# Scores in two passes: the keys as whole-number rows, their scale in the exponential, the maximum's shift brought in by two queues

## The chip, the cores and the metric

One core of one Trainium2 chip. The number is the device time of one execution in microseconds (us), the median over several runs. The engines are TensorE (PE, with its weight load PEld), VectorE (DVE), ScalarE (ACT), GpSimd (POOL) and SyncE (SP), each working through its own instructions in order; SP and ACT can also issue DMAs.

## The reference

32 sequences of 128 tokens out of an alphabet of 28 go through three layers. Only the attention matters here:

```python
h = tok_ref(ids, mask, ...)               # embedding, window feature over 3 tokens, linear map, layernorm
x = _layernorm(h)                         # [B=32, S=128, D=256]
q, k, v = x @ Wq + bq, x @ Wk + bk, x @ Wv + bv        # 16 heads of 64
attn = softmax(q @ k.T / sqrt(64))
y = x + (attn @ v) @ Wo + bo
h = h + layernorm(y, eps=1e-3) * gamma + beta
h = h + ffn_ref(_layernorm(h), ...)       # router over 16 experts, top 2, gelu experts
```

## The kernel before

A token's layernormed row depends only on which token it is and on what stands beside it. So each token is a short row u of 64 numbers: 28 one-hot entries and 28 window shares (together `nb`), both scaled by `r12`, the token's own inverse root, and a few constant columns. `ub` holds these rows transposed for all 32 sequences, as a f16 value and its f16 rest (`ub[:, b, 0]`, `ub[:, b, 1]`), twice over, on partitions 0 to 63 and 64 to 127 (halves `ab` = 0, 1). Queries are `gp` times `ub`, again as value and rest, `qh` and `ql`. Row `SHIFT` of `qh` holds minus the maximum of the query's scores, and row `SHIFT` of the keys' `ub` holds ones, so the shift comes with the product.

The kernel has three stages. Stage 1 builds tables, roots and `ub`. Stage 2 is the attention: one turn `i` of its loop works on several sequences at once. Stage 3 is the feed-forward part. The order on each engine is written out by hand and kept by semaphores. In a turn of stage 2:

- PE: `residual(i)` (L1278), `turn(i+1, 0)`, `values(i+1, 1)`, logits, `q_rows`, `score_cols(i+2, 1)` (L1238), `maxima_cols(i+3)` (L1309), `turn(i+1, 1)`, `q_rows`, `output(i+1, 0)`, `values(i+2, 0)`, `score_rows(i+4, 0)`, `score_cols(i+3, 0)`, `x_cols(i)` (L1287), `output(i+1, 1)`, `score_rows(i+4, 1)`.
- ACT: `max_row(i+3)` (L972: the negated maxima of 16 heads into `mrow`), `exps(i+2, 3)` (L953), `q_hi(i+4, 1)` (L944), `context_hi`, `exps(i+2, 2)`, `probs_hi` twice (L959), `exps(i+3, 1)`, `x_hi(i)` (L976), `exps(i+3, 0)`, `probs_hi` twice, `y_squares(i+1)` (L992).
- POOL: `var_y(i)` (L851, after `y_squares`), `root_y`, `probs_lo`, `h2`, `probs_lo`, `var_x`, `x_rows` (the last is L882, writing `xc`), then `probs_lo` twice.
- SP: waits for `mrow`, then two DMAs (L836), one for each half `ab`, bring 8 heads' maxima each into row `SHIFT` of `qh`.

`score_cols` makes the scores of 4 heads for each half, in three passes: `ub[.., 0]` by `qh`, `ub[.., 0]` by `ql`, `ub[.., 1]` by `qh`. A pass is two matmuls of 512 columns, one on each half of the rows. For `hf` = 0 it waits for the shift's DMAs and for `exps(b-1, 2)` and `exps(b-1, 3)`; `x_cols(b)` waits for `xc`. `exps` gives its bias `ln_r[:, b]` from SBUF and its scale as a constant.

Of the kernel before, what the change touches and what calls it, by code (L numbers as in the profile page):

```python
# [34 lines left out]
V = 28  # L35
# [6 lines left out]
R2, ONE, SHIFT = 2 * V, 2 * V + 1, 2 * V + 2  # L42
ONE_HI, UV = R2 + 2, R2 + 4
# [48 lines left out]
def build(nc, d, out):  # L92
    with ExitStack() as ctx:
# [28 lines left out]
        u_top, u_rest, nk = uh[:, 0], ul[:, 0], uh[:, 1]  # L122
# [45 lines left out]
        uf = sb1("uf", [P, B, UD])  # L168
# [18 lines left out]
        nk_step = sem("nk_step")  # L187
# [12 lines left out]
        UT_BANKS = [psum[n] for n in (2, 3, 6, 7)]  # L200
        TABLE_BANKS = [psum[4], psum[5], psum[4]]
# [16 lines left out]
        with nc.Block() as block:  # L218
# [30 lines left out]
            @block.gpsimd  # L249
            def _(pool):  # L250
                nc.gpsimd.memset(lhs_t[:], 0.0).then_inc(cleared, 1)
                nc.gpsimd.memset(row1[:], 0.0).then_inc(cleared, 1)
                nc.gpsimd.memset(tg[:], 0.0).then_inc(cleared, 1)
                nc.gpsimd.memset(ex[:], 0.0).then_inc(cleared, 1)
                pool.wait_ge(cleared, CLEARED["row_0"])
                nc.gpsimd.memset(row1[:, 0:V], 1.0).then_inc(cleared, 1)
                nc.gpsimd.memset(nb[:, :, 2 * V:UD], 0.0).then_inc(cleared, 1)
                nc.gpsimd.memset(tt[:], 0.0).then_inc(cleared, 1)
                nc.gpsimd.memset(uf[:, :, R2:UD], 0.0).then_inc(cleared, 1)
                nc.gpsimd.memset(mhalf[:], -0.5)  # L260
# [4 lines left out]
                nc.gpsimd.memset(uf[:, :, ONE:SHIFT + 1], 1.0).then_inc(cleared, 1)  # L265
                pool.wait_ge(nt_ready, 4)
# [12 lines left out]
                pool.wait_ge(nk_step, 3)  # L279
                for n, src in ((R2, s1), (ONE_HI, s12)):  # L280
                    nc.gpsimd.tensor_scalar(column(n), src[:], 1.0, 0.0, ALU.mult, ALU.add).then_inc(nk_step, 1)
                pool.wait_ge(nk_step, 5)
                for n, src in ((R2, s1), (ONE_HI, s12)):
                    nc.gpsimd.tensor_tensor(column(n + 1), src[:], column(n), ALU.subtract)

            @block.scalar
            def _(act):
# [15 lines left out]
                act.wait_ge(n_ok, 2)  # L303
                nc.scalar.activation(nk[:, :, 0:2 * V], nb[:, :, 0:2 * V], ACT.Copy)
# [82 lines left out]
            def _(dve):  # L387
# [29 lines left out]
                for n in range(2):  # L417
# [26 lines left out]
                                      twice(psum[7][:, 0:2 * KC * UD].rearrange("p (x u) -> p x u", u=UD))).then_inc(mt_ok, 1)  # L444
                dve.wait_ge(cs_ok, 1)
# [9 lines left out]
                                               op0=ALU.mult, op1=ALU.subtract).then_inc(mr_ok, 1)  # L455

# [91 lines left out]
            def _(pe):  # L548
# [34 lines left out]
                keep_going(15, psum[0][:, 0:FREE])  # L583
# [8 lines left out]
                keep_going(6, psum[0][:, 0:FREE])  # L592
# [57 lines left out]
                def gram():  # L650
                    pe.wait_ge(qkv_ok, 4)
                    for h in range(H):
                        k0 = K * (h % 2)
                        c = (h // 8 * 4 + h // 2 % 2 * 2 + h // 4 % 2) * UD
                        mm = nc.tensor.matmul(psum[h % 2][0:UD, c:c + UD], qkv_t[k0:k0 + K, 0, h // 2, :],
                                              qkv_t[k0:k0 + K, 1, h // 2, :], start=True, stop=True)
                        if h >= H - 2:
                            mm.then_inc(g_ready, 1)

                def z_part(n):  # L660
                    if n == 0:
# [18 lines left out]
                quads(3)  # L680
                table(1)
# [26 lines left out]
        in_cd, gate, g_exp = sem("in_cd"), sem("gate"), sem("g_exp")  # L708
        gate_count, dve_count, steps = [0], [0], {}
# [62 lines left out]
        xc = sb2("xc", [P, 2, D])  # L772

# [54 lines left out]
        with nc.Block() as block:  # L828
            @block.sync
            def _(sp):  # L830
                sp.dma_start(countdown[:], d["countdown"]).then_inc(in_cd, 16)
                for b in range(B):
                    sp.wait_ge(mrow_done, b + 1)
                    for ab in range(2):
                        r = ab * UD + SHIFT
                        sp.dma_start(qh[r:r + 1, b % 2].rearrange("o f t q -> o (f t) q"),  # L836
                                     mrow[8 * ab:8 * ab + 8, b % 2, :]).then_inc(shift_in[b % 2], 16)
# [101 lines left out]
            def _(act):  # L939
# [7 lines left out]
                def exps(b, j):  # L947
# [5 lines left out]
                    nc.scalar.activation(pf[:, j, :], ST[j % 2][:], ACT.Exp, bias=ln_r[:, b:b + 1]).then_inc(exp_done[j], 1)  # L953
# [42 lines left out]
                for i in STEPS:  # L996
# [6 lines left out]
                    if i == -3:  # L1003
                        nc.scalar.preload_act_table(ACT.Exp)
# [38 lines left out]
            def _(dve):  # L1043
# [28 lines left out]
                def sums(b, hf):  # L1072
                    dve.wait_ge(pv_ready[hf], b + 1)
                    step("sum", hf)
                    nc.vector.tensor_reduce(total[:, hf], CB[hf][:].rearrange("p (h u) -> p h u", u=UD)[:, :, ONE_HI:UV], AX.X, ALU.add)\
# [56 lines left out]
                DVE_TOKENS = {(-5, 0): (2,), (-5, 1): (5,), (-5, 2): (8,), (-4, 0): (11,), (-4, 1): (13, 14)}  # L1132

                nc.vector.memset(cn[:].rearrange("p h t (a u) -> p (h t a) u", u=UD)[:, :, UV:UD], 0.0).then_inc(cn_zero, 1)
                for i in STEPS:
                    if has(i + 5):
                        q_lo(i + 5, 1)
                    for n in DVE_TOKENS.get((i, 0), ()):
                        token_rows(n)
                    if has(i + 2):  # L1140
                        context_lo(i + 2, 1)
                    if i == -4:
                        log_rho()
# [43 lines left out]
            def _(pe):  # L1187
# [138 lines left out]

                for i in STEPS:
# [438 lines left out]
```

## Time and profile before

| | |
|---|---|
| median of 3 runs | 538.77 us (538.43 to 546.91) |
| the profiled execution's own time | 537.01 us |
| its span in the profile | 535.2 us |
| PE busy | 497.3 us (93%) |
| DVE busy | 447.9 us (84%) |
| ACT busy | 379.2 us (71%) |
| POOL busy | 384.7 us (72%) |
| granted TensorE clock, mean | 0.989 |

Busy time is summed over all three stages. The span leaves out 1.8 us around the traced work. An instruction that issues a DMA counts as no engine's busy time, though its queue is occupied while it issues.

### The profile page before, as it was taken

What the parts mean: (1) busy time and instruction counts of PE and PEld (TensorE: products, weight loads), DVE (VectorE), ACT (ScalarE), POOL (GpSimd) and SP (SyncE); (2) the same over time, 40 slices, a digit from 0 to 9 for tenths busy, and PEclk for the clock granted to TensorE, in tenths of its full rate; (3) what the DMA queues carried; (4) which work ended last, traced back from release to release, by engine and by line L of the source; (5) the groups of instructions that cost most, each with busy time, mean ns of one, the idle gap of its engine ahead of it and who ended that gap; (6) DMA issues with size and microseconds to landing.
All of it is one profiled execution on the core that took longest, in us unless ns stands there. A gap on an engine that the chain in (4) does not pass through costs nothing. (4 is left out here: it accounts for less than half of the span.)

```text
span 535.2 us, 15239 instructions
## 1 busy us (share of the span) xinstructions
PE 497.3 (93%) x5567; PEld 362.8 (68%) x5567; DVE 447.9 (84%) x1054; ACT 379.2 (71%) x768; POOL 384.7 (72%) x519
## 2 busy tenths in 40 slices
PE   5988799999999999999999998769999999999984
PEld 3876567777777777776777775534466767777664
DVE  4797669999999999998999999868778898878675
ACT  2868778888898888988898887336766555556530
POOL 1025669888788888888888888750468798789783
PEclk9998989999999999999999999999999999999998
DMA  6800000000000000000000000000734163351011
GB/s 233 333 6 2 2 2 4 2 3 3 3 2 3 3 3 3 4 2 4 3 4 2 3 3 2 2 1 4 168 80 100 23 150 76 77 138 38 31 40 60
DMA packets 11902, 21.68 MB, mean 41 GB/s; under 512 B 4668, under 2 KB 9780, under 8 KB 10164
## 3 DMA queue, kind: packets, MB, share of 16 engines
q1 hardware_dynamic: 11410, 20.15, 13.8%
q8 instruction: 45, 0.74, 0.6%
q10 hardware_dynamic: 418, 0.55, 0.4%
q14 instruction: 29, 0.24, 0.2%
HBM read 16.24 MB, written 4.33 MB: 38 GB/s over the span
## 5 line engine op out<-in xcount | busy, mean ns | idle before, releaser
L845 POOL TENSOR_TENSOR s_pl<-s_pf,s_ph 128x512 f16<-128x512 f32 x128 | 147.0, 1160 | 8.7 <-ACT s_ph L959 8.7
L1062 DVE TENSOR_REDUCE s_mx<-ps 128x4 f32<-128x512 f32 x128 | 83.8, 677 | 17.6 <-PE ps L1225 14.1
L953 ACT ACTIVATE s_pf<-ps,s_ln_r 128x512 f32<-128x512 f32 x128 | 87.1, 683 | 11.4 <-PE ps L1238 8.9
L823 PE MATMUL ps<-s_xt_all,s_w1s 128*128 128x512 f16 x384 | 87.9, 379 | 2.2 <-ACT s_ub L1543 1.6
L1698 PE MATMUL ps<-s_w2s,s_hid 128*128 128x256 f16 x768 | 88.9, 273 | 0.0
L1698 PEld LDWEIGHTS ps<-s_w2s,s_hid 128*128 128x128 f16 x768 | 75.1, 98 | 11.0
L959 ACT ACTIVATE s_ph<-s_pf 128x512 f16<-128x512 f32 x128 | 74.0, 637 | 0.0
L1273 PE MATMUL ps<-s_zh,s_cth 128*128 128x256 f16 x256 | 69.9, 273 | 1.0 <-DVE s_ctl L1096 1.0
L1273 PE MATMUL ps<-s_zl,s_cth 128*128 128x256 f16 x256 | 69.8, 273 | 0.0
L1273 PE MATMUL ps<-s_zh,s_ctl 128*128 128x256 f16 x256 | 69.8, 273 | 0.0
L823 PEld LDWEIGHTS ps<-s_xt_all,s_w1s 128*128 128x128 f16 x384 | 37.3, 98 | 41.4 <-ACT s_ub L1543 2.1
L1238 PE MATMUL ps<-s_qh,s_ub 64*128 64x512 f16 x256 | 49.5, 383 | 1.1 <-DMA s_qh<-s_mrow 1.1
L1053 DVE SCALAR_TENSOR_TENSOR s_ql<-ps,s_qh 128x512 f16<-128x512 f32 x64 | 43.4, 679 | 7.4 <-ACT s_qh L944 7.1
L944 ACT ACTIVATE s_qh<-ps 128x512 f16<-128x512 f32 x64 | 38.2, 598 | 13.7 <-PE ps L1212 12.1
L1506 POOL TENSOR_TENSOR s_hid<-s_ub,s_hid 128x512 f16<-128x512 f32 x21 | 25.9, 1253 | 27.8 <-ACT s_hid L1550 27.6
L1096 DVE TENSOR_TENSOR s_ctl<-ps,s_cth 128x512 f16<-128x512 f32 x64 | 43.6, 681 | 0.1
L1087 DVE TENSOR_TENSOR s_cn<-ps,s_rsum 128x480 f32<-128x480 f32 x64 | 41.8, 653 | 1.2
L1212 PE MATMUL ps<-s_ub,s_gp 128*128 128x128 f16 x512 | 40.1, 224 | 1.7 <-PEq L218 1.6
L1264 PE MATMUL ps<-s_ident,s_cn 128*128 128x128 f32 x256 | 38.7, 273 | 2.4 <-DVE s_cn L1087 2.4
L965 ACT ACTIVATE s_cth<-ps 128x512 f16<-128x512 f32 x64 | 38.5, 602 | 2.7 <-PE ps L1264 2.7
L1255 PE MATMUL ps<-s_uh,s_ph 128*128 128x60 f16 x512 | 36.8, 190 | 0.2 <-issue 0.2
L1255 PEld LDWEIGHTS ps<-s_uh,s_ph 128*128 128x128 f16 x512 | 32.3, 97 | 6.9 <-issue 6.7
(246 smaller groups left out, 1149.0 us busy)
## 6 DMA issues: line engine op xcount, KB each, us to landing
s_rep<-picks SPq DMA_DIRECT2D x14, 512.0 KB, 6.7
s_stage<-in_w SPq DMA_DIRECT2D x2, 1024.0 KB, 14.3
out<-s_zh SPq DMA_DIRECT2D x16, 128.0 KB, 2.0
out<-s_lg SPq DMA_DIRECT2D x16, 128.0 KB, 1.7
s_stage<-in_wq SPq DMA_DIRECT2D x1, 1024.0 KB, 5.0
s_stage<-in_wk SPq DMA_DIRECT2D x1, 1024.0 KB, 6.7
s_stage<-in_wv SPq DMA_DIRECT2D x1, 1024.0 KB, 8.3
s_stage<-in_wo SPq DMA_DIRECT2D x1, 1024.0 KB, 10.8
```

Source lines behind the costliest of these rows:

```text
L823: mm = nc.tensor.matmul(hidden_bank(n)[:], w1s[:, wp, c, j * P:(j + 1) * P], xt_all[:, GB * g:GB * (g + 1), xp, c, :], start=(k == 0), sto ...
L845: nc.gpsimd.tensor_tensor(flat(pl[:, b % 2, 4 * j:4 * j + 4, :]), pf[:, j, :], flat(ph[:, b % 2, 4 * j:4 * j + 4, :]), ALU.subtract).then_ ...
L953: nc.scalar.activation(pf[:, j, :], ST[j % 2][:], ACT.Exp, bias=ln_r[:, b:b + 1]).then_inc(exp_done[j], 1)
L959: nc.scalar.activation(flat(ph[:, b % 2, 4 * j:4 * j + 4, :]), pf[:, j, :], ACT.Copy).then_inc(phi_done[j], 1)
L1053: nc.vector.scalar_tensor_tensor(out=flat(ql[:, b % 2, hf]), in0=A[hf][:], scalar=1.0 / G_SCALE, in1=flat(qh[:, b % 2, hf]), op0=ALU.mult, ...
L1062: nc.vector.tensor_reduce(mx[:, b % 2, c:c + 4], A[ab][:].rearrange("p (h k) -> p h k", h=4), AX.X, ALU.max).then_inc(max_done[hf][ab], 1)
L1087: nc.vector.tensor_tensor(cn[:, hf].rearrange("p t (a u) -> p (t a) u", u=UD)[:, :, 0:UV], CB[hf][:].rearrange("p (h u) -> p h u", u=UD)[: ...
L1096: nc.vector.tensor_tensor(flat(ctl[:, b % 2, 4 * hf:4 * hf + 4, :]), CB[hf][:], flat(cth[:, b % 2, 4 * hf:4 * hf + 4, :]), ALU.subtract).t ...
L1238: mm = nc.tensor.matmul(ST[ab][:], ub[r, b, part, :], flat(q[r, b % 2, hf]), start=(n == 0), stop=(n == 2))
L1255: mm = nc.tensor.matmul(CB[hf][:, c:c + UV], p[:, b % 2, h, :], nk[:, b, 0:UV], start=(n == 0), stop=(n == 1))
L1273: nc.tensor.matmul(YB[:, 0:D], c[:, b % 2, p, :], zz[:, p, :], start=(p == 0 and c is cth and zz is zh), stop=False)
L1698: mm = nc.tensor.matmul(zb[b % 4], hid[:, g % 2, hp, j, t * P:(t + 1) * P], w2s[:, wp, j, :], start=False, stop=(j == NJ - 1 and hp == 1))
```

## The change

The keys no longer carry `r12`. A new table `nkT` holds the transposed rows of `nb`, which f16 represents exactly, and is the stationary side of `score_cols`; the pass with the rest of the keys goes. The factor `r12` of the key's token, which is the partition of the scores, is given to `exps` as a scale from SBUF. The constant columns change to match: the rows for the root, the bias and the shift now each appear in the keys as value and rest (`R2`, `R2+1`, `ONE`, `ONE+1`, `SHIFT`, `SHIFT+1`), filled from `nk` by `scale_rows`, one copy and 12 DMAs at the start of stage 2; the shift stands in two rows of `qh` for each half, so there are four DMAs in a turn, two by SP and two by ACT (`shift_rows`, after `exps(i+2, 3)`). `nkT` is made in stage 1 by 64 matmuls, four copies on ACT and four on DVE; 21 filler matmuls (`keep_going`) go. PE's order in a turn stays.

```diff
+                for n in range(4):
+                    act.wait_ge(nt_ready, 4 + n + 1)
+                    nc.scalar.activation(nkT[:, 4 * n:4 * n + 4, :].rearrange("p b t -> p (b t)"), NKT_BANKS[n][:], ACT.Copy)\
+                        .then_inc(nt_ok, 1)
...
+                nc.scalar.activation(nk[:, :, 0:2 * V], nb[:, :, 0:2 * V], ACT.Copy)
                 root_1()
...
+                def nkt_cols(n):
+                    dve.wait_ge(nt_ready, 8 + n + 1)
+                    nc.vector.tensor_copy(nkT[:, 16 + 4 * n:20 + 4 * n, :].rearrange("p b t -> p (b t)"), NKT_BANKS[4 + n][:])\
+                        .then_inc(nkt_ok, 1)
...
-                keep_going(15, psum[0][:, 0:FREE])
+                def nkt_part(n):
...
+                    for k in range(4):
+                        for ab in range(2):
+                            mm = nc.tensor.matmul(NKT_BANKS[n][ab * UD:(ab + 1) * UD, k * P:(k + 1) * P], nb[:, 4 * n + k, :], ident16[:],
+                                                  start=True, stop=True)
...
+                sp.wait_ge(srow_step, 2)
+                for ab in range(2):
+                    for r, j in ((R2, 0), (R2 + 1, 1), (ONE, 2), (ONE + 1, 3), (SHIFT, 2), (SHIFT + 1, 3)):
+                        r += ab * UD
+                        sp.dma_start(nkT[r:r + 1, :, :], srow[:, j, :]).then_inc(in_srow, 16)
                 for b in range(B):
                     sp.wait_ge(mrow_done, b + 1)
-                    for ab in range(2):
-                        r = ab * UD + SHIFT
-                        sp.dma_start(qh[r:r + 1, b % 2].rearrange("o f t q -> o (f t) q"),
-                                     mrow[8 * ab:8 * ab + 8, b % 2, :]).then_inc(shift_in[b % 2], 16)
+                    for r in range(SHIFT, SHIFT + 2):
+                        sp.dma_start(qh[r:r + 1, b % 2].rearrange("o f t q -> o (f t) q"), mrow[0:8, b % 2, :])\
+                            .then_inc(shift_in[b % 2], 16)
...
-                    nc.scalar.activation(pf[:, j, :], ST[j % 2][:], ACT.Exp, bias=ln_r[:, b:b + 1]).then_inc(exp_done[j], 1)
+                    nc.scalar.activation(pf[:, j, :], ST[j % 2][:], ACT.Exp, bias=ln_r[:, b:b + 1], scale=r12[:, b:b + 1]).then_inc(exp_done[j], 1)
...
+                def shift_rows(b):
+                    act.wait_ge(mrow_done, b + 1)
+                    for r in range(UD + SHIFT, UD + SHIFT + 2):
+                        act.dma_start(qh[r:r + 1, b % 2].rearrange("o f t q -> o (f t) q"), mrow[8:16, b % 2, :])\
+                            .then_inc(shift_in[b % 2], 16)
...
                     if has(i + 2):
                         exps(i + 2, 3)
+                    if has(i + 3) and i > -3:
+                        shift_rows(i + 3)
                     if has(i + 4):
                         q_hi(i + 4, 1)
...
-                        pe.wait_ge(shift_in[b % 2], 32 * (b // 2) + 32)
+                        pe.wait_ge(shift_in[b % 2], 64 * (b // 2) + 64)
+                        if b == 0:
+                            pe.wait_ge(in_srow, 16 * 12)
...
-                    for n, (part, q) in enumerate(((0, qh), (0, ql), (1, qh))):
+                    for n, q in enumerate((qh, ql)):
...
-                            mm = nc.tensor.matmul(ST[ab][:], ub[r, b, part, :], flat(q[r, b % 2, hf]),
-                                                  start=(n == 0), stop=(n == 2))
+                            mm = nc.tensor.matmul(ST[ab][:], nkT[r, b, :], flat(q[r, b % 2, hf]),
+                                                  start=(n == 0), stop=(n == 1))
```

The four copies on ACT stand where its copy of `nk` stood, which moves to just before `root_1()`. Of DVE's four (`nkt_cols`), 0 and 1 stand before `cres`, 2 and 3 just before the quads (L462). Of PE's eight `nkt_part`, 6 and 7 stand before `table(0, range(3))`, which is ahead of the quads.

On DVE, `log_rho`, which makes the bias `ln_r`, moves in turn -4 from behind 2 tiles of token rows to the front of the turn, and those token rows move back.

## Rows read from the trace of the kernel before

**Rows 1.** TensorE's timeline over one turn: start, length (us), line, shape, count
```profile
202.37 0.39 PE L1278 MATMUL ps<-s_mr,s_ub 128*128 128x256 f16 x2
...
204.92 0.28 PE L1309 MATMUL ps<-s_ident,s_mx 128*16 128x128 f32 x1
...
208.12 0.38 PE L1238 MATMUL ps<-s_qh,s_ub 64*128 64x512 f16 x2
208.33 0.38 PE L1238 MATMUL ps<-s_ql,s_ub 64*128 64x512 f16 x2
...
208.86 0.44 PE L1287 MATMUL ps<-s_ident,s_xc 128*128 128x128 f32 x2
...
210.87 0.39 PE L1278 MATMUL ps<-s_mr,s_ub 128*128 128x256 f16 x2
```

**Rows 2.** ScalarE's timeline over the same turn
```profile
205.24 0.27 ACT L972 ACTIVATE s_mrow<-ps 16x128 f16<-16x128 f32 x1 [0.36 <-PE ps L1309]
205.41 0.66 ACT L953 ACTIVATE s_pf<-ps,s_ln_r 128x512 f32<-128x512 f32 x1
206.12 0.60 ACT L944 ACTIVATE s_qh<-ps 128x512 f16<-128x512 f32 x1
...
207.09 0.69 ACT L953 ACTIVATE s_pf<-ps,s_ln_r 128x512 f32<-128x512 f32 x1
207.66 1.16 ACT L959 ACTIVATE s_ph<-s_pf 128x512 f16<-128x512 f32 x2
208.97 0.69 ACT L953 ACTIVATE s_pf<-ps,s_ln_r 128x512 f32<-128x512 f32 x1 [0.15 <-PE ps L1238]
209.56 0.38 ACT L976 ACTIVATE s_xt_all<-ps 128x256 f16<-128x256 f32 x1
209.82 0.69 ACT L953 ACTIVATE s_pf<-ps,s_ln_r 128x512 f32<-128x512 f32 x1
...
211.43 0.39 ACT L992 ACTIVATE s_ysq<-ps 128x256 f32<-128x256 f32 x1
```

**Rows 3.** Waits from 100 to 340 us: us in total, times, longest
```profile
POOL s_vy L851 <- ACT s_ysq L992: 28.6, 28, 1.7
...
PEld ps L1238 <- DMA s_qh<-s_mrow: 1.6, 3, 0.6
```

**Rows 4.** GpSimd's timeline over the same turn
```profile
203.50 0.19 POOL L851 TENSOR_SCALAR s_vy<-s_ssy 128x1 f32<-128x1 f32 x1 [0.96 <-ACT s_ysq L992]
...
208.23 0.56 POOL L882 TENSOR_SCALAR s_xc<-s_h,s_negm,s_rx_all 128x256 f32<-128x256 f32 x1 [0.17 <-issue]
```

**Rows 5.** ScalarE groups over the span: count, busy us, mean ns
```profile
L976 ACT ACTIVATE s_xt_all<-ps 128x256 f16<-128x256 f32 x32 | 12.1, 377 | 11.1 <-PE ps L1287 11.0
...
L983 ACT ACTIVATE s_h<-ps,s_sig 128x256 f32<-128x256 f32 x20 | 7.9, 475 | 1.8 <-PE ps L1193 1.8
```

**Rows 6.** SyncE's queue in that turn
```profile
205.53 1.31 SPq L836 DMA_DIRECT2D s_qh<-s_mrow  x2
```

**Rows 7.** The shift transfers' line: issue ns min/median/max, first and last start
```profile
L836 SPq DMA_DIRECT2D s_qh<-s_mrow x64: 634/635/744, 56.2 to 325.7; - x64
```

**Rows 8.** ScalarE and its queue (ACTq) in the first 5 us
```profile
0.73 1.28 ACT L288 ACT_TABLE_LOAD   x1 [0.73 <-PEq L1757]
...
1.75 0.69 ACTq L291 DMA_DIRECT2D s_fus_b<-in_fus_b  x1
3.81 0.37 ACTq L293 DMA_DIRECT2D s_fus_w<-in_fus_w  x1
```

**Rows 9.** The same line from 85 to 340 us
```profile
L836 SPq DMA_DIRECT2D s_qh<-s_mrow x58: 634/635/635, 85.4 to 325.7; - x58
```

**Rows 10.** VectorE from 9 to 30 us
```profile
20.51 1.29 DVE L462 TENSOR_TENSOR s_h<-ps,s_nb 128x512 f32<-128x512 f32 x2 [0.18 <-PE ps L626]
```

**Rows 11.** SyncE's queue in the first 5 us
```profile
1.64 0.43 SPq L223 DMA_DIRECT2D s_iota<-in_iota  x1
...
3.77 0.43 SPq L228 DMA_DIRECT2D s_ident<-in_ident  x1
```

More of the change, by code:

```diff
@@ L41 @@
 UD = 64
-R2, ONE, SHIFT = 2 * V, 2 * V + 1, 2 * V + 2
-ONE_HI, UV = R2 + 2, R2 + 4
+R2, ONE, SHIFT = 2 * V, 2 * V + 2, 2 * V + 4
+UV = ONE + 2
 RHO_SCALE = 0.25
@@ L200, in build @@
         UT_BANKS = [psum[n] for n in (2, 3, 6, 7)]
+        NKT_BANKS = [psum[n] for n in (1, 2, 3, 5, 2, 3, 1, 5)]
         TABLE_BANKS = [psum[4], psum[5], psum[4]]
@@ L444, in _ @@
                                       twice(psum[7][:, 0:2 * KC * UD].rearrange("p (x u) -> p x u", u=UD))).then_inc(mt_ok, 1)
+                def nkt_cols(n):
+                    dve.wait_ge(nt_ready, 8 + n + 1)
+                    nc.vector.tensor_copy(nkT[:, 16 + 4 * n:20 + 4 * n, :].rearrange("p b t -> p (b t)"), NKT_BANKS[4 + n][:])\
+                        .then_inc(nkt_ok, 1)
+                nkt_cols(0)
+                nkt_cols(1)
                 dve.wait_ge(cs_ok, 1)
@@ L455, in _ @@
                                                op0=ALU.mult, op1=ALU.subtract).then_inc(mr_ok, 1)
+                nkt_cols(2)
+                nkt_cols(3)
                 def quads(g):
@@ L581, in _ @@
                         mm.then_inc(nt_ready, 1)
-                keep_going(15, psum[0][:, 0:FREE])
+                def nkt_part(n):
+                    if 1 <= n < 4:
+                        pe.wait_ge(nt_ok, (1, 2, 4)[n - 1])
+                    elif n >= 4:
+                        pe.wait_ge(nt_ok, 4 + (2, 3, 1, 4)[n - 4])
+                    for k in range(4):
+                        for ab in range(2):
+                            mm = nc.tensor.matmul(NKT_BANKS[n][ab * UD:(ab + 1) * UD, k * P:(k + 1) * P], nb[:, 4 * n + k, :], ident16[:],
+                                                  start=True, stop=True)
+                    mm.then_inc(nt_ready, 1)
+                for n in range(4):
+                    nkt_part(n)
                 pe.wait_ge(in_id, 16)
@@ L590, in _ @@
                 tp.then_inc(mt_ready, 1)
[L592 removed]
+                nkt_part(4)
+                nkt_part(5)
                 pe.wait_ge(mt_ok, 1)
@@ L673, in z_part @@
                     mm.then_inc(z_ready, 1)
+                nkt_part(6)
+                nkt_part(7)
                 table(0, range(3))
+                pe.wait_ge(nkt_ok, 2)
                 quads(0)
@@ L1074, in sums @@
                     step("sum", hf)
-                    nc.vector.tensor_reduce(total[:, hf], CB[hf][:].rearrange("p (h u) -> p h u", u=UD)[:, :, ONE_HI:UV], AX.X, ALU.add)\
+                    nc.vector.tensor_reduce(total[:, hf], CB[hf][:].rearrange("p (h u) -> p h u", u=UD)[:, :, ONE:UV], AX.X, ALU.add)\
                         .then_inc(dve_step, 1)
@@ L1137, in _ @@
                         q_lo(i + 5, 1)
-                    for n in DVE_TOKENS.get((i, 0), ()):
-                        token_rows(n)
+                    if i == -4:
+                        log_rho()
+                    elif i < -4:
+                        for n in DVE_TOKENS.get((i, 0), ()):
+                            token_rows(n)
                     if has(i + 2):
                         context_lo(i + 2, 1)
-                    if i == -4:
-                        log_rho()
                     if has(i + 3):
@@ L1300, in logits, with scale_rows @@
                     mm.then_inc(lg_ready, 1)
+                def scale_rows():
+                    for j in range(4):
+                        mm = nc.tensor.matmul(MISC[0:B, j * P:(j + 1) * P], nk[:, :, R2 + j:R2 + j + 1].rearrange("p b o -> p (b o)"),
+                                              identh[:], start=True, stop=True)
+                    mm.then_inc(srow_step, 1)
                 def maxima_cols(b):
+                    if b == 0:
+                        pe.wait_ge(srow_step, 2)
                     for n in range(2):
@@ L1325, in _ @@
                 BETWEEN = {(-4, 0): 10, (-4, 1): 6, (-3, 0): 10, (-3, 3): 6, (-2, 0): 10, (-2, 2): 8}
+                scale_rows()
                 for i in STEPS:
```

37 lines of the change are left out of this document (21 added, 16 removed).

## The prediction, made before the changed kernel had been timed

> **What bounds the kernel now.** I read the timeline of single turns first, engine by engine, then the waits between engines; the busy shares only say that four engines are near their limits at once. In the middle of stage 2 every turn takes the same time: TensorE begins `residual` at 202.37 and again at 210.87, 8.50 us later, with no long gap [rows 1]. So TensorE looks like the bound, and a pass fewer in each `score_cols` like a pure gain. Before believing that, look for closed loops: chains of work that leave an instruction and come back to the same instruction one or two turns later. A turn can't be shorter than the longest of them.
>
> Loop 1, TensorE alone: 8.50 us.
>
> Loop 2 goes through three engines. ScalarE's `y_squares` starts at 211.43, which is 9.06 after the `residual` of 202.37 [rows 1, 2]. GpSimd's L851 waits for `y_squares` in every turn (28 times, 28.6 us) [rows 3], starts 0.57 after it (203.50, with `y_squares` one turn before at 202.93, that is 211.43 less 8.50) [rows 2, 4], and works through to L882, which ends at 208.79; TensorE's `x_cols` starts at 208.86, 5.36 after L851 [rows 1, 4]. From there to the next `residual` it is 2.01 [rows 1]. Two turns from `residual` to `residual` this way: 9.06 + 0.57 + 5.36 + 2.01 = 17.00, or 8.50 a turn. It closes without slack.
>
> Loop 2 also has a floor: `y_squares` can't start before `residual` is done. That is 0.39 for the instruction [rows 1] and some 0.04 to the reader (as the 210.87 one gives 211.26 and ScalarE comes at 211.43, the present wait is ScalarE's own backlog). 0.43 + 0.57 + 5.36 + 2.01 = 8.37. However fast TensorE gets, a turn stays at 8.37 while GpSimd's chain is what it is.
>
> **What the change takes away.** One pass of `score_cols` is 0.21 (208.12 to 208.33) [rows 1]; two of them a turn are 0.43, so loop 1 falls from 8.50 to 8.07. Loop 2 holds `score_cols` nowhere except through ScalarE. All of this gain beyond 8.37 is lost, and up to 0.13 a turn is there to be had, if ScalarE keeps up.
>
> **What it adds to ScalarE, each turn.** Two things.
>
> First the scale from SBUF in four `exps`. No row has an exponential with both operands. The nearest pair is 256 columns out of PSUM: 377 ns with a constant scale (L976), 475 ns with a scale from SBUF (L983) [rows 5], so 0.10 each; the bounds are nothing and 0.10, and I take 0.10.
>
> Second two DMA issues. On SyncE's queue exactly this transfer takes 634 ns of the queue, two take 1.31 [rows 6, 7]. ScalarE's own queue shows three issues of other shapes, 0.37 and 0.69 at its ends; one began at 1.75 while the table load ran on to 2.01 [rows 8], so an issue runs beside the instruction that was dispatched before it, but holds up the one behind. I take 0.655 (the same transfer, half of 1.31), bounds 0.37 and, if both queues go through one generator, 1.31.
>
> Place them. `max_row` starts at 205.24, 2.87 after `residual`; in the new order one pass earlier, 2.66. SyncE's issue comes 0.29 after it (205.53) [rows 2, 6]; ScalarE's waits for the same event, so 2.95, and two issues end at 4.26. `exps(i+2, 3)`, dispatched ahead of them, is hidden beside them (0.66 long, starts 2.83). Queued behind them is `q_hi(i+4, 1)`, at 4.31 instead of 3.75 [rows 2]: 0.56 late. From there ScalarE has no gap: `exps(i+2, 2)` 0.97 behind it (206.12 to 207.09), two `probs_hi`, `exps(i+3, 1)`, `x_hi`, `exps(i+3, 0)`, two `probs_hi`, `y_squares`. The one pause before was 0.15 ahead of `exps(i+3, 1)`, and with the usual overlap of 0.12 of neighbours it is 0.27 that the delay can eat (208.82 to 208.97) [rows 2]. So `y_squares` moves by 0.56 - 0.27 + 3 x 0.10 = 0.59, to 9.65.
>
> Loop 2 in the new kernel: 9.65 + 0.57 + 5.36 + 2.01 = 17.59, or 8.80 a turn.
>
> Loop 3 is new: `score_cols(i+3, 0)` waits for `exps(i+2, 2)`. That starts at 4.31 + 0.97 = 5.28, lasts 0.69 + 0.10, and with 0.05 to the reader TensorE may start at 6.12. Before, TensorE came there at 5.75 (208.12), and the exponential had ended at 5.41. From `score_cols` to `x_cols` it is 0.74 less a pass, 0.53, and 2.01 to the next `residual`: 8.66. Shorter than loop 2, but it grows by the full cost of both issues, where loop 2, over two turns, grows by half.
>
> VectorE is not late: `q_lo(1)` follows `q_hi(1)` and `score_rows(i+4, 0)` waits for it, but that path (4.31 + 0.60 + 0.06 + 0.69 + 0.06 = 5.72, then 0.24 to `score_cols`, 5.96) stays inside loop 3's 6.12.
>
> **The shift's transfers.** Before, TensorE comes to `score_cols(i+3, 0)` 2.59 after the first issue (205.53 to 208.12) and waits for a transfer in 3 turns, 1.6 us in total [rows 1, 3, 6]. Now it comes at 6.12, 3.17 after the issues: the late ones are nearly all absorbed. No credit beyond what the mean turn below holds.
>
> **The sum over stage 2.** Between the issues of 85.4 and 325.7 (the last is the second of its pair, 0.68 behind the first) lie 28 turns [rows 9], 8.56 us each with the late ones: 239.6. New, 28 x 8.80 = 246.4. That is +6.8. In the two or three turns before 85 the loops are shorter and ScalarE has the same two issues; +0.5. The turns after the last issue have neither, and nothing changes.
>
> **The ends.** Stage 1: `nkt_cols(2)` and `(3)` are two 512-column copies on VectorE, just before the quads' first product at 20.51, where VectorE had waited only 0.18 [rows 10]. A 512-column instruction is 0.60 to 0.69 there (1.29 for two). The product is on the chain of roots that everything later needs. So +1.0 (1.29 less the wait and the overlap), bounds 0.5 and 1.3. The other two copies, ScalarE's and the moved copy of `nk`, fill waits; I cost them at nothing, at 0.5 if I am wrong. TensorE's 64 small matmuls take the place of fillers. Stage 2: `scale_rows` before the first query, +0.3. Its 12 transfers hold SyncE's queue for 12 x 0.66 = 7.9 us from about 48 on, and the first shift was issued at 56.2 [rows 7], so they just fit; if a transfer from 32 partitions takes 0.9, +1. The earlier `log_rho` may give back as much in turn -4. I leave both out.
>
> Sum: 6.8 + 0.5 + 1.0 + 0.3 = +8.6. On the profiled execution's 537.01 that is 545.6; its time lies 1.76 under the median, so 547.4.
>
> **Where the Trainium skill speaks against this.** "DMA: Bandwidth & Descriptors", section "Issuing engines are not separate DMA queues", says that starting DMAs from several engines saves only the sequencer's time, usually small. The row speaks otherwise: 634 ns of the queue for 2 KB [rows 7]. The same page's "Anatomy of one DMA", written for GpSimd's path, gives some 50 ns for the dispatch; with that little an issue would delay nothing, and the first rival below would be the outcome. No run here yet shows which holds on ScalarE.
>
> **The rivals.**
>
> *A. The issues are cheap on ScalarE.* For it: the third of its issues took 0.37 [rows 8]. Against: exactly this shape takes 0.63 on the other queue. At 0.37 each, loop 2 is 8.80 - 0.285 = 8.51, and the sum 28 x 8.51 - 239.6 + 1.8 = +0.5: 539.3. If they delay nothing, `q_hi(1)` starts one pass earlier than before, at 3.54; `y_squares` at 8.88, the turn 8.41, the sum -2.3: 536.4.
>
> *B. TensorE is the bound and nothing else.* The turn becomes 8.07: 28 x 8.07 - 239.6 + 1.8 = -11.8, 527.0. Against it: loop 2's floor of 8.37, and L851's wait in all 28 turns [rows 3].
>
> *C. Both queues share what makes the transfers, and so the four issues, which start on one event, take turns.* For it: the issue at 1.75 on ScalarE's queue took 0.69, beside SyncE's of 1.64. Against: the one at 3.81 took 0.37 beside SyncE's of 3.77, and both of SyncE's took the same 0.43 [rows 8, 11]. Its place is loop 3: with 1.31 each instead of 0.655 it is 8.66 + 1.31 = 9.97, the sum 28 x 9.97 - 239.6 + 1.8 = +41.4: 580. Half as much sharing, 0.98 each, gives 9.31 and 561.6. It decides the sign of the verdict from 0.73 each on, where loop 2 is 8.88 and the total passes 2%.
>
> **How the numbers follow.** Forecast case (issues at 0.58 to 0.73, scale 0 to 0.10): 541 to 550, chance 0.54, value 547.4. A: 0.20, 536 to 541. B: 0.05. C: 0.14, 554 to 580. Something in stage 1 or the first turns that I left out, up to +5: 0.07. The range 536 to 563 leaves out B, and the full C. What a measurement of this kernel can tell from no change is about 2%, 10.8 us: faster means under 528, slower over 549.5. The upper part of the forecast's range, C and the last case give slower 0.38; B and a little of A faster 0.06; the rest 0.56.
>
> **What would show each step.** A turn in mid-stage of 8.8; SP and ACT queue rows of 0.63 on the new lines; `q_hi(i+4, 1)` some 1.65 behind `max_row` instead of 0.88; the exponential at 0.78; GpSimd's L851 still waiting for `y_squares`, longer; PE with idle time at `x_cols`, released by `xc`; the quads' first product near 21.5. A turn of 8.37 to 8.5 shows A; 8.07 shows B; issues over 0.9 and TensorE waiting for exponentials or the shift show C. The forecast is wrong above all if ScalarE's queue does not hold up the instruction behind an issue for its full length.

## The result: slower by 1.6%, near the forecast, through two errors that cancel

The changed kernel takes 546.32 us (544.99 to 549.06 in 4 runs) against 538.78 (538.43 to 546.91) for the kernel before: ratio 1.0157, 95% interval 1.0119 to 1.0195. That is slower, by less than the 2% from which the forecast counts a kernel as slower. The forecast was 547.4, range 536 to 563. The profiled execution took 545.84, its span is 544.0; that is +8.8 on before's, where the sum said +8.6.

The page of the changed kernel, its engine line and the group of the exponentials (count, busy us, mean ns):

```profile
PE 492.9 (91%) x5486; PEld 357.7 (66%) x5486; DVE 457.0 (84%) x1059; ACT 389.5 (72%) x773; POOL 386.4 (71%) x519
L991 ACT ACTIVATE s_pf<-ps,s_ln_r,s_r 128x512 f32<-128x512 f32 x128 | 99.6, 781 | 0.7 <-PE ps L1290 0.7
```

Line numbers have moved: `score_cols` is L1290, `residual` L1330, `x_cols` L1339, `exps` L991, `q_hi` L982, `max_row` L1010, the new issues L1015, `y_squares` L1036, GpSimd's L851 and L882 are now L889 and L920.

TensorE's timeline over one turn (start, length, line, shape, count), to be laid beside [rows 1]:

```profile
223.24 0.39 PE L1330 MATMUL ps<-s_mr,s_ub 128*128 128x256 f16 x2
...
225.57 0.28 PE L1369 MATMUL ps<-s_ident,s_mx 128*16 128x128 f32 x1
...
229.54 0.39 PE L1290 MATMUL ps<-s_qh,s_ul 64*128 64x512 f16 x2
229.76 0.39 PE L1290 MATMUL ps<-s_ql,s_ul 64*128 64x512 f16 x2
230.08 0.44 PE L1339 MATMUL ps<-s_ident,s_xc 128*128 128x128 f32 x2
```

`score_cols` has its pass fewer, and comes to `x_cols` sooner. Yet the turn is longer: the `x_cols` before this one started at 221.22, so 8.86 us. ScalarE shows why (ACTq is its DMA queue):

```profile
225.88 0.27 ACT L1010 ACTIVATE s_mrow<-ps 16x128 f16<-16x128 f32 x1
226.06 0.76 ACT L991 ACTIVATE s_pf<-ps,s_ln_r,s_r 128x512 f32<-128x512 f32 x1
226.18 1.41 ACTq L1015 DMA_DIRECT2D s_qh<-s_mrow  x2
227.69 0.60 ACT L982 ACTIVATE s_qh<-ps 128x512 f16<-128x512 f32 x1 [0.87 <-PE ps L1262]
228.18 0.59 ACT L1003 ACTIVATE s_cth<-ps 128x512 f16<-128x512 f32 x1
228.66 0.78 ACT L991 ACTIVATE s_pf<-ps,s_ln_r,s_r 128x512 f32<-128x512 f32 x1
229.32 1.16 ACT L997 ACTIVATE s_ph<-s_pf 128x512 f16<-128x512 f32 x2
230.36 0.79 ACT L991 ACTIVATE s_pf<-ps,s_ln_r,s_r 128x512 f32<-128x512 f32 x1
...
232.99 0.41 ACT L1036 ACTIVATE s_ysq<-ps 128x256 f32<-128x256 f32 x1
```

`q_hi` starts 1.81 behind `max_row`, where [rows 2] had 0.88. The bracket blames TensorE's L1262, whose last product had ended at 226.86. What really ended just before 227.69 is the second issue (226.18 + 1.41 = 227.59): the profile infers releasers from semaphores, and the end of an issue on the engine's own queue is none, so the idle time is put down to the last semaphore. From there on ScalarE works without a gap, the pause of [rows 2] ahead of the third exponential is eaten, and `y_squares` starts 9.75 behind `residual` (9.06 before). GpSimd waits for it longer. Waits of the changed kernel from 100 to 340 us (total, times, longest), against [rows 3], and GpSimd's own two starts in that turn, against [rows 4]:

```profile
POOL s_vy L889 <- ACT s_ysq L1036: 34.1, 27, 1.3
ACT s_qh L982 <- PE ps L1262: 22.6, 26, 1.0
...
PEld ps L1339 <- POOL s_xc L920: 12.6, 27, 1.5
```
```profile
224.73 0.19 POOL L889 TENSOR_SCALAR s_vy<-s_ssy 128x1 f32<-128x1 f32 x1 [1.25 <-ACT s_ysq L1036]
229.45 0.56 POOL L920 TENSOR_SCALAR s_xc<-s_h,s_negm,s_rx_all 128x256 f32<-128x256 f32 x1 [0.17 <-issue]
```

Loop 2 with these numbers: 9.75 + 0.59 + 5.35 + 2.01 = 17.70, 8.85 a turn. Forecast: 8.80. That such a sum gives the turn proves nothing: distances read from one trace, from an instruction back to itself two turns later, always add up to two turns, whatever bounds them. What speaks for loop 2 is that 8.80 was worked out from the other kernel, and that each of its links waits for the one before: GpSimd for `y_squares` in every turn, ScalarE without a gap, `x_cols` 0.07 behind the end of `xc` (229.45 + 0.56 = 230.01).

Loop 3, which the forecast had at 8.66, is in fact as long. `score_cols` starts 0.10 behind the end of the exponential that it waits for (228.66 + 0.78 = 229.44, then 229.54) and `x_cols` 0.54 behind `score_cols`. In 25 turns of mid-stage the first distance is 0.10 in all but one (0.30, a late transfer) and the second 0.54 in all, and no kernel with two passes shows less of either (0.53 once). From `residual`: 2.65 + 1.80 + 0.97 + 0.78 + 0.10 + 0.54 + 2.01 = 8.85. In the next turn the pair of issues takes 0.09 more, and it shows which of the two loops sets such a turn. ScalarE, TensorE and GpSimd:

```profile
235.03 1.50 ACTq L1015 DMA_DIRECT2D s_qh<-s_mrow  x2
236.64 0.60 ACT L982 ACTIVATE s_qh<-ps 128x512 f16<-128x512 f32 x1 [0.97 <-PE ps L1262]
...
237.61 0.78 ACT L991 ACTIVATE s_pf<-ps,s_ln_r,s_r 128x512 f32<-128x512 f32 x1
```
```profile
238.49 0.39 PE L1290 MATMUL ps<-s_qh,s_ul 64*128 64x512 f16 x2
...
239.03 0.44 PE L1339 MATMUL ps<-s_ident,s_xc 128*128 128x128 f32 x2
```
```profile
238.31 0.56 POOL L920 TENSOR_SCALAR s_xc<-s_h,s_negm,s_rx_all 128x256 f32<-128x256 f32 x1 [0.17 <-issue]
```

`q_hi` is 1.90 behind `max_row` (234.74) and the turn 8.95: the longer issue is paid in full, in the same turn. `score_cols` is again 0.10 behind its exponential, and `x_cols` now 0.16 behind the end of `xc`, so it didn't wait for GpSimd. In the usual turn the two loops are level to 0.02 or so.

The issue lines over the whole span (ns min/median/max), ScalarE's pair and SyncE's, against [rows 7]:

```profile
L1015 ACTq DMA_DIRECT2D s_qh<-s_mrow x64: 627/744/1100, 56.0 to 332.9; - x64
L874 SPq DMA_DIRECT2D s_qh<-s_mrow x64: 625/629/698, 56.0 to 332.9; - x64
```

Where the 8.8 us lie, by milestones read from both timelines (us from the start):

| milestone | before | after | difference |
|---|---|---|---|
| first product of the quads | 20.51 | 21.50 | +0.99 |
| `max_row(0)` | 55.88 | 55.73 | -0.15 |
| first exponential | 62.50 | 61.35 | -1.15 |
| `max_row(3)` | 85.13 | 82.98 | -2.15 |
| `max_row(31)` | 324.73 | 331.97 | +7.24 |
| last `x_cols` of stage 2 | 354.8 | 362.7 | +7.9 |
| first product of stage 3's experts | 390.4 | 399.2 | +8.8 |
| end of the span | 535.2 | 544.0 | +8.8 |

So the 28 turns from `max_row(3)` to `max_row(31)` cost 9.4 instead of 6.8, and the start of stage 2, which I had at +0.5, gave back over 2 us.

The giving back shows first in one bracket. ScalarE's first exponential in the kernel before and in the changed one:

```profile
62.50 1.26 ACT L953 ACTIVATE s_pf<-ps,s_ln_r 128x512 f32<-128x512 f32 x2 [2.33 <-DVE s_ln_r L1069]
```
```profile
61.35 1.45 ACT L991 ACTIVATE s_pf<-ps,s_ln_r,s_r 128x512 f32<-128x512 f32 x2 [0.28 <-PE ps L1290]
```

Before, it sat 2.33 us for VectorE's `log_rho`; now only 0.28, for TensorE.

### The profile page after: what moved, and what is told of

Read it like the earlier page. It is cut to its first block and busy times, and to the rows that moved or that the text cites. A ratio compares the mean times of both kernels' runs of the same rounds, so it can differ in the third digit from the quotient of the medians.

```text
span 544.0 us, 15165 instructions
## 1 busy us (share of the span) xinstructions
PE 492.9 (91%) x5486; PEld 357.7 (66%) x5486; DVE 457.0 (84%) x1059; ACT 389.5 (72%) x773; POOL 386.4 (71%) x519
## 5 line engine op out<-in xcount | busy, mean ns | idle before, releaser
L991 ACT ACTIVATE s_pf<-ps,s_ln_r,s_r 128x512 f32<-128x512 f32 x128 | 99.6, 781 | 0.7 <-PE ps L1290 0.7
L1325 PE MATMUL ps<-s_zh,s_ctl 128*128 128x256 f16 x256 | 69.8, 273 | 0.0
L1325 PE MATMUL ps<-s_zl,s_cth 128*128 128x256 f16 x256 | 69.8, 273 | 0.0
L982 ACT ACTIVATE s_qh<-ps 128x512 f16<-128x512 f32 x64 | 38.1, 597 | 29.6 <-PE ps L1262 27.2
L1316 PE MATMUL ps<-s_ident,s_cn 128*128 128x128 f32 x256 | 40.2, 280 | 3.0 <-DVE s_cn L1134 2.8
L1262 PE MATMUL ps<-s_ub,s_gp 128*128 128x128 f16 x512 | 38.6, 219 | 0.0
L1307 PE MATMUL ps<-s_uh,s_pl 128*128 128x60 f16 x512 | 36.8, 190 | 0.0
```

Of the source, the lines that this page charges most:

```text
L1307: mm = nc.tensor.matmul(CB[hf][:, c:c + UV], p[:, b % 2, h, :], nk[:, b, 0:UV], start=(n == 0), stop=(n == 1))
L1316: tp = nc.tensor.transpose(CB[hf][:, t * P:(t + 1) * P], cn[:, hf, t, :], ident[:])
L1325: nc.tensor.matmul(YB[:, 0:D], c[:, b % 2, p, :], zz[:, p, :], start=(p == 0 and c is cth and zz is zh), stop=False)
```

## The experiments

Ratios are to the kernel before, each with its 95% interval. "Turn" is the median distance of `x_cols` in the profiled execution over the 28 turns. "To `q_hi`" is how far `q_hi(i+4, 1)` starts behind `max_row`, the median of the same turns. The kernel before was timed again beside each group of experiments (medians 537.5 to 538.4), and each ratio goes by the runs of its own group: compare the ratios, not the times. The edits shown are shortened.

| kernel | time, us | ratio | turn, us | to `q_hi`, us |
|---|---|---|---|---|
| before | 538.78 | 1 | 8.50 | 0.88 |
| changed | 546.32 | 1.0157 (1.0119 to 1.0195) | 8.86 | 1.80 |
| 1 scale constant | 544.17 | 1.0129 (1.0082 to 1.0175) | 8.68 | 1.72 |
| 2 four issues on SyncE | 560.15 | 1.0402 (1.0324 to 1.0480) | 9.29 | 0.96 |
| 3 issues apart | 541.33 | 1.0059 (1.0026 to 1.0093) | 8.65 | 1.03 |
| 4 `log_rho` late | 547.71 | 1.0225 (1.0159 to 1.0290) | 8.86 | 1.80 |
| 5 two rows a transfer | 538.23 | 1.0019 (0.9986 to 1.0052) | 8.52 | 1.04 |
| 6 ... and a third pass | 546.22 | 1.0136 (1.0082 to 1.0189) | 8.68 | 0.88 |
| 7 ... and GpSimd's chain cut | 554.91 | 1.0303 (1.0258 to 1.0348) | 8.99 | 1.04 |
| 8 one row, SyncE alone | 535.11 | 0.9958 (0.9931 to 0.9985) | 8.47 | 0.96 |
| 9 ... and scale constant | 533.46 | 0.9909 (0.9869 to 0.9949) | 8.35 | 0.96 |
| 10 before, `log_rho` early | 534.45 | 0.9945 (0.9924 to 0.9966) | 8.50 | 0.88 |

**1. The scale operand by itself.**

```
-  activation(pf[:, j, :], ST[j % 2][:], ACT.Exp, bias=ln_r[:, b:b + 1], scale=r12[:, b:b + 1])
+  activation(pf[:, j, :], ST[j % 2][:], ACT.Exp, bias=ln_r[:, b:b + 1])
```

> The changed kernel with the exponentials' scale a constant again; the factor of the key's token is left out of the scores. Theory (ScalarE's queue in loop 2, two turns long): three of the four exponentials lie between the queue's issues and y_squares, 0.10 each, so a turn falls from 8.86 by 0.15 to 8.71 and the time by some 4 us to 542. Rival (the shift's transfers or GpSimd alone set the turn): the turn stays at 8.86 and the time at 546.

The exponentials' group of this kernel:

```profile
L991 ACT ACTIVATE s_pf<-ps,s_ln_r 128x512 f32<-128x512 f32 x128 | 88.0, 690 | 0.9 <-PE ps L1290 0.8
```

0.09 less each, and the turn fell by 0.18, more than the 0.15 expected. The rest is in the issues, which the edit leaves alone: `q_hi` starts 1.72 behind `max_row` instead of 1.80, as the second issue took 0.67 in the median instead of 0.75. Loop 2 holds three exponentials and this 0.08 over two turns (0.18 a turn), loop 3 one exponential and the 0.08 in each turn (0.17), so the experiment doesn't tell the loops apart. The time fell by only 2 us where the turns are worth 4 to 5: in its profiled execution TensorE's granted clock was at half (1.2 GHz) in two stretches near 17 and 48 us, which the changed kernel's doesn't have. The turn is the cleaner reading.

**2. ScalarE's issues put on SyncE.**

```
-  for r in range(SHIFT, SHIFT + 2):                                  (and shift_rows on ScalarE)
+  for ab in range(2):
+      for r in range(ab * UD + SHIFT, ab * UD + SHIFT + 2):
           sp.dma_start(qh[r:r + 1, ...], mrow[8 * ab:8 * ab + 8, ...])
```

> All four transfers of the shift issued by SyncE, none by ScalarE. Theory: ScalarE is free, but the fourth transfer is issued 2.0 later than the first and lands 1.7 after that, so TensorE waits for it at score_cols: 2.95 + 2.0 + 1.7 = 6.65 after residual, then 0.53 and 2.01 to the next residual, a turn of 9.2 and a time of 556. Rival (only the queue time taken from ScalarE mattered): a turn of 8.4 to 8.5, 535.

ScalarE is free again (`q_hi` at 0.96), and yet the turn is the longest of all ten. SyncE's line, who waits for it, and TensorE in one turn:

```profile
L875 SPq DMA_DIRECT2D s_qh<-s_mrow x128: 634/635/690, 55.3 to 344.2; - x128
...
  PEld ps L1282: 26.9, 32
```
```profile
225.76 0.39 PE L1282 MATMUL ps<-s_qh,s_ul 64*128 64x512 f16 x2 [0.64 <-DMA s_qh<-s_mrow]
```

Four issues one behind the other take 2.67, and `score_cols` waits for the last in every turn. So ScalarE's queue is the lesser evil here: with two issues in each queue the transfers landed some 0.6 before `score_cols` in the changed kernel, with four in one queue they come last.

**3. The two issues apart, `q_hi(1)` between them.**

```
+                    if has(i + 3) and i > -3:
+                        shift_rows(i + 3, (0,))
                     q_hi(i + 4, 1)
-                        shift_rows(i + 3)          (stood ahead of q_hi)
+                        shift_rows(i + 3, (1,))
```

> The changed kernel, with ScalarE's two issues parted: one after exps(i+2, 3) as now, one after q_hi(i+4, 1), so that each runs beside an instruction already dispatched. Theory (an issue holds up only what is queued behind it, while what was dispatched before it goes on): the work behind is late by 0.45 less, loop 2 shorter by half of it, a turn of 8.63 and 540. Rival (an issue takes its time from the engine wherever it stands): 8.86 and 546.

ScalarE and its queue in one turn:

```profile
223.54 0.27 ACT L1010 ACTIVATE s_mrow<-ps 16x128 f16<-16x128 f32 x1
223.71 0.76 ACT L991 ACTIVATE s_pf<-ps,s_ln_r,s_r 128x512 f32<-128x512 f32 x1
223.84 0.63 ACTq L1015 DMA_DIRECT2D s_qh<-s_mrow  x1
224.57 0.60 ACT L982 ACTIVATE s_qh<-ps 128x512 f16<-128x512 f32 x1
224.59 0.63 ACTq L1015 DMA_DIRECT2D s_qh<-s_mrow  x1
225.32 0.60 ACT L1003 ACTIVATE s_cth<-ps 128x512 f16<-128x512 f32 x1 [0.16 <-issue]
```

Each issue now runs beside the instruction dispatched ahead of it: the first beside an exponential, the second beside `q_hi`. `q_hi` comes 1.03 behind `max_row`, and 0.16 of idle time is left behind the second issue. `exps(i+2, 2)` starts 2.28 behind `max_row`; that was 2.77 with the two issues in a row, and is 1.93 with none on ScalarE (experiment 8). So the pair costs this queue 0.84 in a row and 0.35 apart. Turn and time fell as expected: 0.21 a turn, 5 us in all, for one issue moved. The turns now alternate, 8.47 and 8.83 by turns for much of the stage. That is the mark of a loop two turns long, loop 2; loop 3 would be 8.35 with this kernel's distances.

**4. `log_rho` back where it was.**

```
-  if i == -4:
-      log_rho()                          (first in turn -4)
...
+  if i == -4:
+      log_rho()                          (behind the two low parts)
```

> The changed kernel with log_rho and the token rows on VectorE back in their old order in turn -4. The first exponential came 1.15 earlier in the changed kernel than before, max_row of sequence 1 came 2.4 earlier. If the order did that, both go back and the time rises by 1.2 to 2.4, to 547.5 to 548.7. If it was the granted TensorE clock, which stood at half speed for two stretches of 3.4 us between 46 and 70 us in the kernel before and in none of them in the changed one, nothing moves.

The first exponential in this kernel:

```profile
62.61 1.45 ACT L991 ACTIVATE s_pf<-ps,s_ln_r,s_r 128x512 f32<-128x512 f32 x2 [2.12 <-DVE s_ln_r L1116]
```

The wait for `log_rho` is back and the turns are unchanged. A stretch of half clock on TensorE (65.9 to 69.3) stands in this profile too, as in that of the kernel before (66.5 to 69.9). As a time, 547.71 against 546.32 is too little for these few runs; experiment 10 measures it better.

**5. Two rows in each transfer, SyncE alone.** The maxima lie twice in `mx` and `mrow`, so one issue fills both rows.

```
+  nc.vector.tensor_copy(v[:, :, 1, :], v[:, :, 0, :])      (VectorE, once a turn)
-  for r in range(SHIFT, SHIFT + 2):  dma_start(qh[r:r + 1, ...], mrow[0:8, ...])
+  for ab in range(2):                dma_start(qh[r:r + 2, ...], mrow[16 * ab:16 * ab + 16, ...])
```

> The maxima stand twice in mx (one small copy on VectorE, 0.2 a turn, in a gap), so that one transfer fills both shift rows of a half: two transfers a turn, both by SyncE, none by ScalarE; same results. Theory: q_hi(1) is back at 3.54 after residual, y_squares at 8.88, loop 2 gives 8.41 a turn; against the changed kernel's 8.86 and 28 turns some 13 us less, 533, that is 5 under the kernel before. Rival (the scale operand and the transfers cost what was lost, not ScalarE's queue): 8.7 or more, 542. Second rival: TensorE was the bound after all, 8.07, 524.

8.52, not 8.41. The copy on VectorE costs more than it looks, because it stands ahead of `cn`, which TensorE wants next. VectorE and TensorE in one turn:

```profile
203.45 0.20 DVE L1109 COPY s_mx<-s_mx 128x16 f32<-128x16 f32 x1
203.79 0.66 DVE L1133 TENSOR_TENSOR s_cn<-ps,s_rsum 128x480 f32<-128x480 f32 x1
```
```profile
204.25 0.28 PE L1369 MATMUL ps<-s_ident,s_mx 128*32 128x128 f32 x1
204.50 0.66 PE L1317 MATMUL ps<-s_ident,s_cn 128*128 128x128 f32 x4
```

The transposes of `cn` start 0.25 behind that of the maxima, where it is 0.12 in the kernel before and 0.13 in experiment 8, `y_squares` comes 9.11 behind `residual`, and (9.11 + 0.57 + 5.36 + 2.01) / 2 = 8.52. My 8.41 had left the copy at nothing.

**6. The same with the third pass put back** (`ub`'s rest by `qh`, as before the change: a product of the same length that these keys don't need).

> e5 with the third pass put back (the rest of the keys by qh, which is now nearly nothing and of no use). Theory: without ScalarE's issues a pass is worth only what loop 2's floor leaves: 8.07 + 0.43 = 8.50 for TensorE alone, 8.52 for loop 2, so 0.11 a turn and 3 us over e5, 536. Rival (TensorE sets the turn, two passes are 0.43): 12 us over e5.

Two passes a turn, 0.43 us of TensorE's time, cost 0.16. That is the measured price of what the change removes, where TensorE alone would say 0.43; and at 8.68 this kernel isn't on TensorE's own 8.50 either. The passes act through ScalarE, whose exponentials wait for `score_cols`. That wait between 100 and 340 us (total, times, longest), here and in experiment 5:

```profile
ACT s_pf L992 <- PE ps L1291: 7.7, 28, 0.9
```
```profile
ACT s_pf L992 <- PE ps L1291: 1.3, 3, 0.6
```

The time rose by 8 us, more than 28 x 0.16 = 4.5; two half-speed stretches of the clock (66.4 to 69.8 and 397.5 to 400.9) lie in this profile, and what of the rest they explain wasn't separated.

**7. GpSimd's chain cut by one small instruction.** The negation L911 goes, L921 subtracts instead of adding the negative.

```
-  tensor_scalar(negm[:, p:p + 1], mvx[:, b, 0:1], -1.0, 0.0, ALU.mult, ALU.add)
-  tensor_scalar(xc[:, p, :], tok[:, b, :], negm[:, p:p + 1], rx_all[:, b:b + 1], ALU.add, ALU.mult)
+  tensor_scalar(xc[:, p, :], tok[:, b, :], mvx[:, b, 0:1], rx_all[:, b:b + 1], ALU.subtract, ALU.mult)
```

> e5 with one of GpSimd's small instructions gone: the negated mean is no longer made, L920 subtracts the mean itself. It was 0.15 of GpSimd's chain, which loop 2 passes once in two turns and its floor once a turn. Theory: 8.33 to 8.26 a turn, 2 to 4 us under e5, 530. Rival (GpSimd's chain isn't in what sets the turn): as e5.

It went the other way. The instruction in experiment 5, then in this one:

```profile
207.88 0.55 POOL L921 TENSOR_SCALAR s_xc<-s_h,s_negm,s_rx_all 128x256 f32<-128x256 f32 x1 [0.17 <-issue]
```
```profile
206.01 1.22 POOL L919 TENSOR_SCALAR s_xc<-s_h,s_mvx,s_rx_all 128x256 f32<-128x256 f32 x1
...
207.29 0.44 PE L1338 MATMUL ps<-s_ident,s_xc 128*128 128x128 f32 x2 [0.54 <-POOL s_xc L919]
```

As an edit it failed; as a test it is the strongest of the study, in the other direction. `var_y` to `x_cols` is 5.98 now instead of 5.36, and `y_squares` starts 0.45 behind `residual`, at its floor. The floor worked out from the kernel before, 8.37, with the 0.62 added to GpSimd's chain gives 8.99. Measured: 8.99. GpSimd's chain sets this turn one for one, while TensorE has work for 8.07.

**8 and 9. One row shifted in each half, two issues on SyncE; then the constant scale as well.** These two give what the change would be without its cost on ScalarE: 8 leaves the shift's rest out of the scores, 9 the key's factor as well.

```
-  for r in range(SHIFT, SHIFT + 2):  dma_start(qh[r:r + 1, ...], mrow[0:8, ...])
+  for ab in range(2):                dma_start(qh[ab * UD + SHIFT:..., ...], mrow[8 * ab:8 * ab + 8, ...])
```

> The changed kernel with one shift row for each half, as before the change: SyncE issues two transfers a turn, ScalarE none, VectorE makes no copy. The shift's rest row is left out of the scores. In e5 the copy moved VectorE's cn, and with it turn(i+1, 1) and q_hi(1), by 0.14. Theory: without it q_hi(1) is at 3.54 after residual, loop 2 gives 8.41 a turn against e5's 8.53, 3 us less, 535. Rival (the copy had nothing to do with it): 8.53 and 538.

> e8 with the exponentials' scale a constant too: of what the change put on ScalarE nothing is left, while TensorE still has the two passes. The factor of the key's token and the shift's rest are left out of the scores. Theory: loop 2 over two turns would be 8.26, its floor with GpSimd's chain is 8.37, so 8.37 a turn and 534. Rival (TensorE alone is what remains): 8.07, 525.

8.47 and 8.35. In the last, `y_squares` starts 0.43 behind the `residual` of its turn: loop 2 stands on its floor, 8.37 as worked out before the change was timed, and not on TensorE's 8.07. By that floor less work on ScalarE or in `score_cols` can take a turn no lower.

**10. The kernel before, with `log_rho` first in turn -4 and nothing else.**

> The kernel before with nothing changed but VectorE's turn -4: log_rho first, its token rows later. e4 undid this in the changed kernel: the first exponential came 1.9 later, counted from the first quad product. Theory: the same here the other way round, turns of 8.50 as before and 1 to 2 us less, 537. Rival: it moves nothing in the kernel before, 538.8.

```profile
60.93 1.27 ACT L953 ACTIVATE s_pf<-ps,s_ln_r 128x512 f32<-128x512 f32 x2 [0.49 <-PE ps L1239]
```

The first exponential comes 1.57 earlier than in the kernel before, and `max_row(3)` at 81.76 instead of 85.13: 3.4 us. Of these some 1.8 lie between the first exponential and `max_row(3)`, where the kernel before has a stretch of half clock (66.5 to 69.9) that this one doesn't have. In time that is 3.0 us (1.8 to 4.1, by the ratio). Part of it is clock: of the kernel before's runs beside the experiments only four had a mean granted clock of 0.995, and took 535.1 to 536.1; of the 12 here seven had it, and took 531.9 to 535.2, 1.1 us less by the medians. It computes what the kernel before does, and it is faster than both kernels.

## Why the forecast held, and where it was wrong

**The bound.** Right in the main: not TensorE, but a loop over several engines. The forecast's "it closes without slack" was no evidence, as such a sum always closes. The evidence is what was worked out beforehand: loop 2 at 8.80 for the changed kernel (8.86 measured), its floor of 8.37 (experiment 9: 8.35), that floor with GpSimd's chain 0.62 longer, 8.99 (experiment 7: 8.99). Two passes, 0.43 of TensorE's time, were worth 0.16 (experiment 6). That in the kernel before both loop 1 and loop 2 hold at 8.50 wasn't tested by itself. Rival B needed 8.07; even with every added cost gone the turn stayed at 8.35.

**The scale operand.** Forecast 0.10 each, measured 781 - 683 = 98 ns; it costs 0.12 to 0.18 a turn (experiments 8 to 9, and changed to 1, where the issues became shorter too).

**The issues on ScalarE: right in kind, under-sized.** That an issue runs beside the instruction dispatched before it and holds the one behind is what experiment 3 shows from one side and experiments 2 and 8 from the other (`q_hi` at 0.96 with no issue on ScalarE). I took 0.655 for each. The first takes 0.63 to 0.65, the second 0.75 as a rule, up to 1.10: pairs of 1.40 to 1.41, not 1.31, and 1.49 to 1.50 in every fourth turn. That is 0.10 of the 9.75 against 9.65, and 0.05 of a turn. Of 9.4 against 6.8, 28 x 0.06 = 1.7 is the typical turn. The other 0.9 is a few long ones, which I had called absorbed: 9.14, 9.15 with a late transfer, 9.21 with the issue of 1.10, and six of 8.95 with the longer pair, less a short last one of 8.39.

**Rival A (cheap issues)** fell: no issue took under 627 ns, and the second of a pair 0.75 in the median. The Trainium skill's "DMA: Bandwidth & Descriptors", section "Issuing engines are not separate DMA queues", calls the sequencer time that a second issuing engine saves usually small relative to the DMA itself. In this kernel it is not small: experiment 2 spends it on one queue and loses 0.43 a turn against the changed kernel. The other side, the compute that two issues in a row hold up behind them on ScalarE, is 0.21 a turn by experiment 3.

**Rival C (shared generator)** fell as a threat: with four issues on one event SyncE's kept their 0.63 and ScalarE's second grew by 0.1. The two queues ran side by side. Why the second one grows wasn't isolated; it took 0.67 with the exponential's scale a constant (experiment 1) and 0.63 with `q_hi` between the two (experiment 3), so SyncE's queue beside it isn't the whole of it.

**Loop 3: under-sized by 0.19, and level with loop 2.** The forecast had 8.66 and "shorter than loop 2"; it is 8.85. `q_hi` came 1.80 behind `max_row` and not 1.65, and `score_cols` 0.10 behind the exponential and not 0.05. So a turn of 8.86 has two bounds, and part of the agreement with 8.80 is that they are equally long. It matters for the price of an issue: more of it costs the turn in full (0.09 more gave 8.95), less of it is worth about half (0.49 off the start of `exps(i+2, 2)` gave 0.21, experiment 3), as loop 2 then holds. The transfers were no part of either; they landed some 0.6 before `score_cols`.

**Stage 1.** Forecast +1.0 at the quads' product, measured +0.99. To two digits that is luck: with the same stage 1 and no stretch of half clock there, experiments 2, 4, 6 and 8 have the product at 20.77 to 21.63, and experiment 10, with the old one, at 20.97 where the kernel before has 20.51.

**The first turns: wrong, and the largest miss.** I wrote that the earlier `log_rho` may give back as much as the transfers cost and left both out, without asking who waits for it. ScalarE did, 2.33 us, in a row of the timeline that was read before the forecast and not used. I had +1.8 at `max_row(3)` (1.0 + 0.3 + 0.5); it was -2.15, 3.9 away. Experiment 10 shows 3.4 of that in a kernel with nothing else changed. The clock is part of it: at half speed at 46.0 to 49.4 and 66.5 to 69.9 before, at neither after. The order of `log_rho` isn't a rule for it: both kernels with the late one (before, experiment 4) have a stretch near 66, but of those with the early one experiment 6 has it as well (66.4 to 69.8). The one near 46 to 48 came and went in the same way. What would pin the clock by itself wasn't tried.

**Stage 3.** +0.9 between the last `x_cols` and the experts' first product, which I had at nothing. It recurs: 35.6 us in the kernel before and in experiment 10, 36.0 to 37.5 in all kernels with the change. TensorE sat idle ahead of that product for 1.39 in the changed kernel and 0.41 before; in the changed one VectorE had waited 1.39 for a transfer into `rep` at 387.59. Why it comes later there stays open.

So the sum was right to 0.2 us (8.6 against 8.8) because two errors of 2.6 and 3.9 stood against each other, and 1.6 us of small ones beside them: 0.6 in the last turns and the 0.9 of stage 3. The match also hangs on which execution was profiled: the one before had a mean clock of 0.989, the changed one 0.997. Against the four runs of the kernel before at 0.995 (535.1 to 536.1) the changed kernel's three at 0.995 to 0.998 (545.0 to 546.8) are some 10 us longer. The reading to trust is the turn, 8.80 against 8.86, with what is said above of its two loops.

## What to carry to other kernels

Before crediting a removed pass on the busiest engine, close the loops: follow the chain from an instruction back to itself through all engines, over as many turns as it takes. That its parts add up to the turn says nothing; look at each link for slack, that is, whether its distance is the least that occurs in any turn, and work out what an edit would give before running it. Loops that come out within some 0.2 us of each other, as 8.80 and 8.66 did, can both bind. Price a DMA issue as an instruction of its engine, here 0.63 to 0.75 us, and put it right behind an instruction of that length that is already dispatched, one issue to each: two in a row held the work behind them up by 0.84, apart by 0.35. Every reordering at a loop's head deserves a look at who waits for what is moved: here, `log_rho` moved forward on VectorE's queue was worth some 3 us, part of it clock.

## What the runs showed of the hardware that I had not expected

GpSimd's two-operand instruction on 128x256 takes 0.55 us as add and multiply on `negm`, and 1.22 as subtract and multiply on a column of `mvx` (experiments 5 and 7); whether the operation or the place of the operand does it wasn't separated. ScalarE's second issue in a row takes 0.75 beside a SyncE issue that takes 0.63, and the longest took 1.10. The profile books the 0.87 of idle time behind a pair of issues to a semaphore that had come 0.8 before.
